# The third normalisation of each sequence moved from VectorE to GpSimd in a one-core decoder block

## What is computed

```
x = x + attention(layernorm(x))                    # 16 heads, causal
x = x + cross_attention(ctx, ctx, layernorm(x))    # one head
x = x + experts(layernorm(x))                      # top 2 of 8 experts, plus one shared expert
layernorm(x) = (x - mean(x)) / sqrt(var(x) + 1e-5)
```

## Time and profile before

| | |
|---|---|
| Median of three runs | 520.73 us (518.72 to 522.56) |
| Profiled execution, own time | 523.42 us |
| Its span (first to last record) | 521.7 us |
| Granted TensorE clock, mean | 0.945 of full |
| Busy: PE, DVE, ACT, POOL | 447.5, 387.7, 320.9, 282.5 us |
| Steady part of the pipeline | about 87 to 280 us |
| Last slots of the pipeline | to about 346 us |

### The profile page before, as it was taken

One profiled execution on the slowest core, in us unless ns is written; L12 is line 12 of the kernel. 1 busy time (PEld: TensorE's weight loads), 2 busy tenths in 40 slices (PEclk: granted clock), 3 DMA queues, 4 the chain that ended last, 5 costly groups with the idle time before them and its releaser, 6 DMA issues.

```text
span 521.7 us, 12081 instructions
## 1 busy us (share of the span) xinstructions
PE 447.5 (86%) x3494; PEld 348.2 (67%) x3494; DVE 387.7 (74%) x1262; ACT 320.9 (62%) x975; POOL 282.5 (54%) x369
## 2 busy tenths in 40 slices
PE   1566999999999999999899978459799999898993
PEld 1344667777677677677677756348588877787783
DVE  4473677788988988979889886878467766566585
ACT  1133778888778779788887867542355544454530
POOL 6604263362584775756755666446156655555581
PEclk9967999999999999999999999568899999999997
DMA  6612222221222222222222312512133322222194
GB/s 184 159 38 55 53 57 59 52 64 48 68 70 65 73 72 58 77 66 65 77 59 72 83 41 92 156 37 85 47 83 90 84 81 82 71 76 81 53 355 122
DMA packets 66998, 43.13 MB, mean 83 GB/s; under 512 B 9211, under 2 KB 63878, under 8 KB 66934
## 3 DMA queue, kind: packets, MB, share of 16 engines
q1 hardware_dynamic: 61876, 33.04, 23.6%
q0 software_dynamic: 4320, 8.99, 5.3%
q10 hardware_dynamic: 738, 0.33, 0.2%
HBM read 17.39 MB, written 12.09 MB: 57 GB/s over the span
## 4 chain that ended last, share of the span: by engine, by line
PE 43%; DVE 24%; DMA 11%; issue 8%; SPq 5%; ACT 4%; POOL 3%; DVEq 0%; ACTq 0%; POOLq 0%
PE ps_scores L809 6%; DMA ys<-ctx_t,late 5%; DVE negmax L1128 5%; DMA late<-xs 4%; PE ps_shared L634 3%; PE ps_shared L826 3%; PE ps_shared L678 3%; PE ps_scores L652 3%; PE ps_scores_t L668 3%; PE ps_scores L653 3%; PE ps_shared L622 3%; SPq L415 2%; DMA k_slots<-qk_stack 2%; PE ps_shared L817 2%; PE ps_shared L686 2%
## 5 line engine op out<-in xcount | busy, mean ns | idle before, releaser
L551 POOL TENSOR_SCALAR_AFFINE_SELECT probs<-probs 128x512 f32<-128x512 f32 x128 | 79.9, 635 | 93.6 <-ACT probs L911 92.4
L1128 DVE TENSOR_REDUCE negmax<-ps_scores 128x4 f32<-128x512 f32 x128 | 86.4, 683 | 24.7 <-PE ps_scores L653 24.4
L574 POOL DMA_INDIRECT ys<-ctx_t,late x71 | 68.4, 963 | 61.2 <-ACT ctx_t L1009 58.7
L911 ACT ACTIVATE probs<-ps_scores_t 128x512 f32<-128x512 f32 x128 | 74.4, 596 | 10.4 <-PE ps_scores_t L668 9.5
L544 POOL DMA_INDIRECT xs<-xrow,posu x64 | 65.1, 1017 | 24.8 <-DVE rsum L1250 13.5
L653 PE MATMUL ps_scores<-k_slots,qk_stack 96*128 96x512 f32 x128 | 78.0, 612 | 0.0
L809 PE MATMUL ps_scores<-wide,qk_stack 128*128 x213 | 69.5, 436 | 0.0
L668 PE MATMUL ps_scores_t<-wide,qk_stack 97*128 97x512 f32 x128 | 58.6, 464 | 1.1 <-issue 1.1
L652 PE MATMUL ps_scores<-causal,ident 128*128 128x512 bf16 x128 | 51.1, 399 | 7.8 <-DMA k_slots<-qk_stack 7.6
L1334 DVE COPY probs<-ps_shared 128x256 f32<-128x256 f32 x71 | 30.2, 425 | 25.3 <-PE ps_shared L817 25.3
L999 ACT ACTIVATE qk_stack<-ps_scores_t 128x128 fp32r<-128x128 f32 x71 | 19.7, 278 | 45.9 <-PE ps_scores_t L801 45.9
(11 more groups left out here) (229 smaller groups left out, 1163.9 us busy)
## 6 DMA issues: line engine op xcount, KB each, us to landing
k_slots<-qk_stack SPq DMA_DIRECT2D x128, 48.0 KB
wide<-qk_stack SPq DMA_DIRECT2D x128, 48.0 KB
late<-xs SPq DMA_DIRECT2D x71, 66.0 KB
wide<-ys SPq DMA_DIRECT2D x8, 512.0 KB, 7.4
ctx_t<-in_ctx SPq DMA_DIRECT2D x32, 64.0 KB, 2.0
out_x<-res SPq DMA_DIRECT2D x8, 256.0 KB, 3.4
ys<-ctx_t,late POOLq DMA_INDIRECT x71, 2.2
wd<-in_L_ffn_w_down SPq DMA_DIRECT2D x8, 128.0 KB, 3.5
```

Of the source, the lines that this page charges most:

```text
L551: pool.affine_select(out=part, in_=part, compare_op=ALU.is_ge, fill=0.0, base=0, pattern=[[0, HJ], [1, T]], channel_multiplier=-1).then_in ...
L574: pool.indirect_dma_start(out=ys, out_offset=bass.IndirectOffsetOnAxis(ap=xload_i[:, i % XL, C + 1:C + 2], axis=0), in_=ybuf[:, i % 4, :], ...
L911: act.activation(probs[:, b % 2, j * HJ:(j + 1) * HJ, :].rearrange("p a t -> p (a t)"), PT[j % 2][:], ACT.Exp)\
L1128: dve.reduce_max(negmax[:, b % 2, j * HJ:(j + 1) * HJ], PS[j % 2][:].rearrange("p (i t) -> p i t", i=HJ), axis=AX.X, negate=True).then_inc ...
```

## The change

`norm_ffn` is taken out of DVE's stages and put into POOL's, with the same operands, waits and semaphore. `ORDER` is unchanged, so POOL runs it behind `attn_out` (L557) and ahead of `norm_x` and the second scatter.

```diff
@@ gpsimd @@
+            def norm_ffn(b):
+                g, u = b // GB, b % GB
+                w.ge(x2_rstd, b + 1)
+                w.ge(scattered[g % 2][u], 16 * 2 * (g // 2))
+                pool.tensor_scalar(xrow[:, g % 2, 0, u, 0:C], res[:, b, :], mv3[:, 0:1], rs3[:, 0:1], ALU.subtract, ALU.mult)\
+                    .then_inc(xn3_ready, 1)
+
...
-            w.run({"norm_x": norm_x, "scores_t": scores_t,
+            w.run({"norm_x": norm_x, "norm_ffn": norm_ffn, "scores_t": scores_t,
                    "attn_out": attn_out, "scatter": scatter, "weights": weights})
@@ vector @@
-            def norm_ffn(b):
-                g, u = b // GB, b % GB
-                w.ge(x2_rstd, b + 1)
-                w.ge(scattered[g % 2][u], 16 * 2 * (g // 2))
-                dve.tensor_scalar(xrow[:, g % 2, 0, u, 0:C], res[:, b, :], mv3[:, 0:1], rs3[:, 0:1], ALU.subtract, ALU.mult)\
-                    .then_inc(xn3_ready, 1)
-
...
-                       scores=scores, tall_sums=tall_sums, attn_out=attn_out, norm_xattn=norm_xattn, norm_ffn=norm_ffn, xscores=xscores,
+                       scores=scores, tall_sums=tall_sums, attn_out=attn_out, norm_xattn=norm_xattn, xscores=xscores,
```

## The result

| | before | after |
|---|---|---|
| Median (range), four runs each | 520.53 us (518.72 to 522.56) | 527.69 us (525.71 to 530.38) |
| Ratio, 95% interval | | 1.0119 (1.0065 to 1.0173) |
| Profiled execution, own time / span | 523.42 / 521.7 us | 525.71 / 524.0 us |
| Busy: PE, DVE, ACT, POOL | 447.5, 387.7, 320.9, 282.5 us | 444.7, 383.0, 320.6, 318.5 us |

Slower by 1.2%. The forecast was 0.8% faster, with a range of 513.3 to 522.0 us and a chance of 0.06 for slower by over 1%. That belongs to the result too.

The account below looks back on a forecast made before the run. PE nearly full with DVE close behind, neither bounding alone. Gains of 1.2 (slot B), 2.3 (slot C) and 0.5 us (last slots) sum to 4.0: from a median of 520.7 to 516.7 us, 8-in-10 range 513.3 to 522.0.

Parts of the forecast that it names:

- The length p: Duration of POOL's new normalisation instruction: taken as 0.40 us, with 0.28 and 1.27 as ends.
- slot D: Slot where PE holds the chain: no gain; DVE's halves come later, but PE starts on time up to 0.70 us.
- slot C: Slot where DVE's L1159 gets through sooner; PE can use 0.46 us, five times: 2.3 us gained.
- slot B: Slot with the removed DVE instruction on the chain: 0.23 us gained, five times, 1.2 us.
- last slots: Two more L1166 on the chain outside the periods, near 304 and at 330.82 us: 0.25 us each, 0.5 us gained.
- New waits: Paragraph on POOL's added waits and later masks: x2_rstd and xn3_ready free, 0.4 us covered by the masks' wait for ACT.
- The section on the port: POOL's new read holds back two-input DVE instructions: small routing ones in slot A, the halves L1116 in slot D.
- The 1.01 us of issue: Chain's issue time at L1166 in slot C, held behind POOL's L557 and L483; to be gone after the change.
- Slot 34: L1159 stuck 2.38 us with POOL's memset: either 0.4 us longer or some 1.7 us gained; nothing counted.
- rival (3): More: slot 34's stall goes (1.7 us) and slot A's 0.9 us come too; 514.1 us, chance 0.14.
- Keys (1): SP's key copies land late for PE in slot B, leaving 0 to 1.5 us; about 520.0 us, chance 0.20.
- Slower (2): POOL's instruction takes 1.27 us, halves in slot D late, PE 0.57 us late five times; 522.9 us, chance 0.10.

Follow-up runs that it names:

- e1: Changed kernel with POOL waiting for the end of its own last mask ahead of each mask; ratio to the kernel before 0.9946.
- e3: Kernel before, normalisation still on DVE, plus a dummy tensor_scalar of the same shape on POOL at the change's place; ratio 1.0116.
- e9: Kernel before with 24 lone POOL instructions added at its end, each waited for; the normalisation's form had a mean of 792 ns.
- e4: Changed kernel with POOL normalising only the first 8 of 128 columns; ratio to the kernel before 0.9911.
- e16: Kernel before with POOL's gaps between masks and ahead of L483, on the 522.6 us chip; ratio to the kernel before 0.9944.
- e15: Changed kernel with one gap only, ahead of POOL's third mask, on the 522.6 us chip; ratio to the kernel before 0.9945.
- e11: Kernel before with POOL waiting for its own last mask ahead of each mask, nothing else; ratio to the kernel before 0.9970.
- e12: Changed kernel with POOL waiting for its own last mask ahead of each mask, on the 541.1 us chip; ratio 0.9871.
- e10: Changed kernel again, unaltered, on the chip where the kernel before takes 541.1 us; ratio 1.0012.
- e14: Changed kernel a third time, unaltered, on the chip where the kernel before takes 522.6 us; ratio 1.0104.

## Why the prediction was wrong

**The length p.** The term was mis-sized: 0.40 us taken, 0.79 measured (e1, e3, e9). The two nearest rows, a mask at 0.284 and an add at 0.464, were taken as neighbours in cost because they have the same shape; the form with two operations and scalars per partition costs more than the two-input add. 0.79 lies inside the ends of 0.28 and 1.27. By the forecast's own rules 0.79 would still have been a gain: slot D 5 x (0.79 - 0.70) = 0.45 lost, slot C 5 x (220.02 - 219.73) = 1.45, slot B 1.2, last slots 0.5, in sum 2.7 us faster. So p alone isn't the error. It is half of it: at 0.39 us (e4) the kernel is 4.0 us faster, and the step below fails at the real length.

**The step that failed** is the cover of "New waits": "The masks wait for ACT (3.31 us idle before those of slot A), so 0.4 us is covered". (The other cover of that paragraph, 0.8 us for the first normalisation in slot C, held: `xT_hi` comes 0.32 us sooner after L557, not later.) Slot A's slack was read for all slots; in B and D it was 1.26 and 1.16 us. In slot C POOL had 0.42 us between the second and the third mask and nothing ahead of the first, and this gap was what let `xT_lo` in. Being late used it up: the masks came in a run, and a DVE instruction that the forecast never looked at was held for 1.76 us more. The section on the port priced the new instruction's own reads, not the old reads that it would shift. In the forecast's words, the cover was gone and the cost was the run.

**Slot C.** From the start of L557 to that of `xT_hi` it was 5.10 us before (217.44 to 222.54) and is 4.78 after (220.39 to 225.17): 0.32 us gained of the 0.46 forecast. `xT_lo` then loses 1.76, and PE's clock 1.2 to 1.5 in some periods. The 1.01 us of issue is gone as said, but `xn` (L1166, new count) is held instead, 1.22 us, up to the end of L483.

**Slots A, B, D together.** The period without the stall is 0.58 us shorter, where slots B and C were to give 0.69. This part of the mechanism was right. In slot D PE starts no later. But it is the reverse of the forecast's picture, as the timeline shows: DVE's halves keep their 1.26 us and POOL is held, which is also why L563's mean is 1017 ns. The rows had it: the halves started at 227.80, 0.09 us before L557 ended, so DVE was there first. The limit of p = 0.70 in slot D has nothing behind it.

```profile
233.66 1.26 DVE L1123 TENSOR_TENSOR qk_lo<-early,qk_hi 128x512 fp32r<-128x512 f32 x2
233.73 1.78 POOL L563 TENSOR_SCALAR xrow<-res,mv,rs 128x128 f32<-128x128 f32 x1
```

**Slot 34.** The stall of 2.38 us is gone, as rival (3) had it: `xn` at 332.38 us takes 0.34, ahead of the memset at 333.82. It couldn't outweigh the rest.

**The rivals.** Keys (1): PE waits for them only where everything else has become shorter (0.5 us in one period of e16). Slower (2): the right sign with the wrong place; its price sat in slot D and needed p above 1.05. None of the rivals had the masks.

**Still open:** why the clock falls behind one 1.9 us wait and not behind the next, what holds ACT's copy on the slower chips, and what the move itself is worth once DVE is let in: nothing on one chip (e15, e16), up to 1.0% on another (e11, e12).

## What to carry to other kernels

Before an instruction is moved to an engine with room, list every later instruction of that engine that it makes late, and look in the slot at hand (not in another one) at which gap between them lets another engine in; an idle gap of 0.4 us can be what a neighbour lives on. Where two engines exclude each other, a wait of one for its own last result, placed inside a run of its instructions, took 7.0 and 8.2 us off the changed kernel (e10 to e12, e14 to e15); on the same two chips moving the work had cost nothing and 5.1 us. And profile the kernel before on the chip on which its rival is timed: half of a ratio is the kernel before.

## What the runs showed of the hardware that I had not expected

- POOL's `tensor_scalar` with two operations and scalars per partition: 0.39 us for 128x8 (e4), 0.79 for 128x128 fp32, so 3.3 ns a column ((0.79 - 0.39) / 120) on a fixed part of about 0.36 us (0.39 - 8 x 0.0033). One operation with a constant takes 0.54, a two-input add of the same shape 0.45. The Trainium skill, "GPSIMD Engine Reference", section "Engine selection", has one-input work roughly at line rate; the measurement is against it here.
- DVE's two-input instruction was held over three POOL instructions of a back-to-back run of four (2.45 us), not over one, and the fourth then waited for it (1.09 us instead of 0.63). A semaphore wait between two of them, about 0.2 us ((3.38 - 2.85) / 3), shortened the hold: 1.29 us with one gap ahead of the third, none with a wait ahead of each. In e4 the DVE instruction took 1.18 us in three of four slots without such a wait; why isn't shown.
- It goes the other way too: POOL's 0.79 us became 1.78 beside two 0.63 us instructions of DVE.
- An idle of 1.92 us of PE was followed in some periods by some 2 us at a clock of 0.50 (229 to 231 us in the changed kernel; its mean over 2 us), and in others by none (192 to 194 us in e14, at 1.00).
